# The experts' LayerNorm and routing moved into the attention's block, and dispatch's plan moved ahead of the places

## The reference

```python
x = x + _L0_attn_ref(_layernorm(x), Wq, bq, Wk, bk, Wv, bv, Wo, bo)
x = x + _L0_ffn_ref(_layernorm(x), gate_w, w_gate_proj, w_up_proj, w_down_proj)
x = x + _L1_attn_ref(_layernorm(x), w_in, w_param, w_out)
x = x + _L1_ffn_ref(_layernorm(x), lut, gate_idx, up_idx, down_idx)

# _L0_ffn_ref
router_logits = x @ gate_w.T
sel_w, sel_e = jax.lax.top_k(router_logits, 8)
masked = jnp.zeros((T, E)).at[rows, sel_e].set(softmax(sel_w))
h = silu(einsum('th,eih->tei', x, w_gate_proj)) * einsum('th,eih->tei', x, w_up_proj)
out = einsum('tei,ehi->th', h * masked[:, :, None], w_down_proj)
```

## Time and profile before

| | us |
|---|---|
| median of 3 runs (2475.92 to 2478.18) | 2477.4 |
| profiled execution, device time | 2489.67 |
| its span | 2488.2 |
| busy of the span: PE / DVE / ACT / POOL | 2283.7 / 1454.8 / 973.4 / 1083.1 |
| last addition of the projection ends | 606.5 |
| norm, first statistics to last low part | 622.1 to 650.9 |
| route, to the end of the mask | 651.7 to 671.9 |
| dispatch, to `token_of` | 672.2 to 708.6 |
| first transpose of the experts | 718.3 |

### The profile page before, as it was taken

The page is one execution under the profiler, slowest core; times in us unless marked ns, Lnnn a source line. Parts: engine busy times, 40 slices in busy tenths (PEclk is TensorE's granted clock), DMA queues, the critical chain, the costliest instruction groups (busy, mean ns, idle before and its releaser), DMA issues. The chain is left out here.

```text
span 2488.2 us, 45641 instructions
## 1 busy us (share of the span) xinstructions
PE 2283.7 (92%) x12486; PEld 1749.9 (70%) x12488; DVE 1454.8 (58%) x3393; ACT 973.4 (39%) x2177; POOL 1083.1 (44%) x976
## 2 busy tenths in 40 slices
PE   7989999967569999999999499999899998999998
PEld 5865555535359989988889278887766665788886
DVE  6446666634655555555555458998076665654554
ACT  3126666541444444444444332222365553312111
POOL 3128778877036666666667111111176662000000
PEclk9989999988679999999999699999999999999999
DMA  5469999987559999999998625456497841000001
GB/s 183 124 186 350 343 353 357 367 314 280 218 164 249 286 285 254 251 282 268 255 241 141 186 87 177 165 174 211 138 252 183 201 102 39 13 26 26 25 10 68
DMA packets 256541, 487.08 MB, mean 196 GB/s; under 512 B 32369, under 2 KB 149489, under 8 KB 246674
## 3 DMA queue, kind: packets, MB, share of 16 engines
q1 hardware_dynamic: 190418, 267.84, 35.2%
q0 software_dynamic: 62976, 212.42, 30.5%
q10 hardware_dynamic: 3024, 5.29, 0.6%
HBM read 588.77 MB, written 198.66 MB: 316 GB/s over the span
## 5 line engine op out<-in xcount | busy, mean ns | idle before, releaser
L1502 PE MATMUL m_ps_u<-m_ring,m_xT_hi 128*128 x1280 | 370.5, 350 | 0.7 <-issue 0.7
L1470 POOL DMA_INDIRECT expert_sum<-x_res,token_of x160 | 258.5, 1616 | 191.2 <-ACT x_res L1573 71.7
L1502 PEld LDWEIGHTS m_ps_u<-m_ring,m_xT_hi 128*128 128x128 f32 x1280 | 236.8, 190 | 1.8 <-issue 1.2
L845 ACT ACTIVATE probs<-ps_c 128x512 f32<-128x512 f32 (+3 forms) x384 | 176.7, 491 | 137.0 <-PE ps_c L771 94.3
L1502 PE MATMUL m_ps_u<-m_ring,m_xT_lo 128*128 x640 | 217.0, 339 | 0.0
L1463 POOL DMA_INDIRECT m_xg<-x_rows,token_of x160 | 171.4, 1072 | 85.1 <-issue 76.0
L1949 PE MATMUL s_ps<-s_x_hi,s_w_hi 128*128 128x512 f32 x512 | 200.4, 391 | 3.1 <-POOL s_w_lo L1919 3.0
L1949 PE MATMUL s_ps<-s_x_hi,s_w_lo 128*128 128x512 f32 x512 | 199.9, 391 | 0.0
L1949 PE MATMUL s_ps<-s_x_lo,s_w_hi 128*128 128x512 f32 x512 | 199.8, 390 | 0.0
L2718 DVE TENSOR_TENSOR x_res<-f_ps_o,x_res 128x512 f32<-128x512 f32 x176 | 109.3, 684 | 143.0 <-PE f_ps_o L2611 143.0
L1521 PE MATMUL m_ps_y<-m_ring,m_hT_hi 128*128 x480 | 176.6, 422 | 11.0 <-issue 11.0
(11 more groups left out here) (360 smaller groups left out, 5636.3 us busy)
## 6 DMA issues: line engine op xcount, KB each, us to landing
m_ring<-w_split SPq DMA_DIRECT2D x160, 1536.0 KB
m_ring<-w_split SPq DMA_DIRECT2D x160, 768.0 KB
w_split<-e_gu_parts POOLq DMA_DIRECT2D x32, 1536.0 KB, 7.5
proj<-s_out SPq DMA_DIRECT2D x32, 1024.0 KB, 3.9
e_raw_gu<-w_experts POOLq DMA_DIRECT2D x32, 768.0 KB
w_split<-e_dn_parts POOLq DMA_DIRECT2D x32, 768.0 KB, 7.1
e_raw_dn<-w_experts POOLq DMA_DIRECT2D x32, 512.0 KB
q_st<-q_parts SPq DMA_DIRECT2D x32, 256.0 KB, 6.3
```

The lines of the kernel that those rows point to most:

```text
L845: nc.scalar.activation(probs[a][j % RING][:, :width], ps_c[(j * BATCH + a) % BUFS][:, :width], ACT.Exp, scale=SCALE).then_inc(exp_done, 1)
L1470: pool.indirect_dma_start(acc[j % 2], rows_at(j), y[j % TURNS], None, bounds_check=PADDED - 1, oob_is_err=True, compute_op=ALU.add).then_i ...
L1502: last = nc.tensor.matmul(ps_u[b % 2][:, :W_UP], x[b % 2][:, k, :], ring[:, first + k * GU_ROW:][:, bass.ds(place, W_UP)], start=(n == 0), ...
```

## The change

The norm's own block goes. A new function, `project_and_normalize`, takes the place of `output_projection` in the attention's block: statistics of a group are taken between the steps of the next one, groups 0 and 1 are also normalized there, and the turning of all 16 tiles follows the last step, into three buffers that are the projection's own `ps_n`. The normalized rows lie in `m_xg`. `route` adds its code to the same block, with waits where a block's end stood, and the attention's semaphores are cleared behind it. In dispatch the plan is made before the places, the routing weights after the first marks, and their store is issued by ScalarE instead of SyncE.

```diff
@@ project_and_normalize, VectorE
+                if k == 0 and g >= 2:
+                    moments(g - 2)
+                if k == 1 and g > 0:
                     add(g - 1)
+                if k == 1 and g >= 2:
+                    scales(g - 2)
+                if k >= 2 and g > 0:
+                    for i in range(2):
+                        tile_stats((g - 1) * SUB + (k - 2) * 2 + i)
             low_part(len(STEPS) - 1)
-            add(GROUPS - 1)
+            moments(LAST - 1)
+            add(LAST)
+            scales(LAST - 1)
+            for i in range(TILES):
+                low_x(i)
+                if i < SUB:
+                    tile_stats(LAST * SUB + i)
...
@@ ScalarE
+                if at == 0 and group >= 2:
+                    deviations(group - 2)
+                if at >= 2 and group >= 2:
+                    for i in range(2):
+                        normalize((group - 2) * SUB + (at - 2) * 2 + i)
+            deviations(LAST - 1)
+            for i in range(TILES):
+                act.wait_ge(transposed, i + 1)
+                nc.scalar.copy(x_hi[:, :, toks(i)], ps_x[i % BUFS]).then_inc(x_hi_done, 1)
+                if i < SUB:
+                    normalize((LAST - 1) * SUB + i)
...
@@ TensorE
+            def turn(i):
+                pe.wait_ge(xn_ready, i + 1)
+                if i >= BUFS:
+                    pe.wait_ge(x_lo_done, i - BUFS + 1)
@@ route
         def _(pool):
+            pool.wait_ge(normalized.transposed, TILES)
+            pool.wait_ge(normalized.rows_stored, rows_stored_all)
             pool.memset(zeros[:, :], 0.0).then_inc(constants, 1)
...
+            pe.wait_ge(normalized.gw_lo_done, 1)
+            pe.wait_ge(normalized.x_lo_done, TILES)
...
+            dve.wait_ge(normalized.rows_stored, rows_stored_all)
             nc.vector.tensor_single_scalar(chosen[:, :, :], rest[:, :, :], TAKEN, ALU.is_equal)
@@ dispatch, ScalarE (and the same two lines gone from SyncE)
+                if i == 2:
+                    act.wait_ge(weighted, 4)
+                    act.dma_start(x_rows[:N_TOK, D:].rearrange("(n p) e -> p n e", p=P), routing[:, :, :]).then_inc(weights_stored, 16)
@@ mixture_of_experts
+            normalized = project_and_normalize(nc, block, sem, attended, x_res, ident, x_hi, x_lo, xn, gate_wT, gw_hi, gw_lo, x_rows[:, :D])
+            route(nc, block, sem, normalized, x_res, x_hi, x_lo, gw_hi, gw_lo, weight, chosen, ident, zeros, acc, x_rows, acc_ready, pads_ready)
+            attention_block.close()
```

More of the change, by code:

```diff
@@ L79, in load_tokens @@
     return x_loaded
[L82 to L223, removed]
-                    last.then_inc(transposed, 1)
@@ L227, in attention @@
-def attention(nc, x_in, x_res, x_loaded, ident, w, b_qk, b_v, wo, bo, w_raw, w_split):
+Attended = namedtuple("Attended", "yT all_sums wo_hi wo_lo wo_split in_chunk in_head of_head quarters y sums")
+def attention(nc, block, sem, x_in, x_res, x_loaded, ident, w, b_qk, b_v, wo, bo, w_raw, w_split):
     qk = {n: nc.dram_tensor(f"{n}_parts", (HEADS, 2, DH, 2 * BATCH + 1, GROUP), F32).ap()[:, :, :, :2 * BATCH, :].rearrange("h a d (s b) t -> h a d s b t", s=2) for n in "qk"}
@@ L256, in attention @@
                v_pair, probs, y_st, raw_wo, neg_max, both_max, max_cols, ident, ident_r, ident_bf, mask, mask_T, marks, warm)
-        output_projection(nc, block, sem, x_res, ident, yT, all_sums, wo_hi, wo_lo, wo_split, in_chunk, in_head, of_head, [q_0, q_1, k_0], probs)
+        quarters = [t[:, half, a, :] for t in (k_1, q_1, q_2) for half in range(2) for a in range(BATCH)]
+        y = [probs[0][0], probs[0][1], probs[0][2], probs[1][3]]
+        return Attended(yT, all_sums, wo_hi, wo_lo, wo_split, in_chunk, in_head, of_head, quarters, y, probs[1][2])
 Projected = namedtuple("Projected", "lo_done v_added hi_stored lo_stored stores k_sem k_count first_free all_done store_rest")
@@ L934, in _, with project_and_normalize @@
             evacuate(BODIES - 1, E - 1, 1)
-def output_projection(nc, block, sem, x_res, ident, yT, all_sums, wo_hi, wo_lo, wo_split, in_chunk, in_head, of_head, spare, spare_rows):
+Normalized = namedtuple("Normalized", "transposed x_lo_done gw_lo_done rows_stored")
+def project_and_normalize(nc, block, sem, attended, x_res, ident, x_hi, x_lo, xn, gate_wT, gw_hi, gw_lo, rows_out):
     SUB = GROUP // P
@@ L954, in output_projection @@
         ps_o = [ctx.enter_context(nc.psum_tensor(f"o_ps_o{b}", [P, D], F32)) for b in range(OUTS)]
+        ps_x = [t[:, :].rearrange("p (k t) -> p k t", k=KD) for t in ps_n]
         loaded = [sem(f"o_loaded{b}") for b in range(Y_BUFS)]
@@ L991, in project_tile @@
                     last.then_inc(step_done, 1)
+            def turn(i):
+                pe.wait_ge(xn_ready, i + 1)
+                if i >= BUFS:
+                    pe.wait_ge(x_lo_done, i - BUFS + 1)
+                for k in range(KD):
+                    last = nc.tensor.transpose(ps_x[i % BUFS][:, k, :], xn[:, i, k * P:(k + 1) * P], ident[:, :])
+                last.then_inc(transposed, 1)
             pe.wait_ge(rows_marked, 3)
@@ L1016, in _ @@
                 take_chunks(g)
-            for n, (group, _) in enumerate(STEPS):
+            for n, (group, at) in enumerate(STEPS):
                 act.wait_ge(y_ready, n + 1)
@@ L1044, in add, with tile_stats, moments, scales @@
                     nc.vector.tensor_tensor(x_res[:, i, :], ps_o[i % OUTS][:, :], x_res[:, i, :], ALU.add).then_inc(added, 1)
+            def tile_stats(i):
+                dve.wait_ge(added, i + 1)
+                nc.vector.bn_stats(stats[:, i, :], x_res[:, i, :]).then_inc(stats_done, 1)
+            def moments(g):
+                dve.wait_ge(stats_done, (g + 1) * SUB)
+                for i in range(g * SUB, (g + 1) * SUB):
+                    nc.vector.bn_aggr(mv[:, i, :], stats[:, i, :]).then_inc(aggregated, 1)
+                dve.wait_ge(aggregated, (g + 1) * SUB)
+                nc.vector.tensor_scalar_add(var_eps[:, of_group(g)], mv[:, of_group(g), 1], LN_EPS).then_inc(var_done, 1)
+            def scales(g):
+                dve.wait_ge(std_done, g + 1)
+                nc.vector.reciprocal(rstd[:, of_group(g)], std[:, of_group(g)]).then_inc(rstd_done, 1)
+                dve.wait_ge(rstd_done, g + 1)
+                nc.vector.scalar_tensor_tensor(shift[:, of_group(g)], mv[:, of_group(g), 0], -1.0, rstd[:, of_group(g)], ALU.mult, ALU.mult).then_inc(shift_ready, 1)
+            def low_x(i):
+                dve.wait_ge(x_hi_done, i + 1)
+                nc.vector.tensor_tensor(x_lo[:, :, toks(i)], ps_x[i % BUFS], x_hi[:, :, toks(i)].bitcast(F32), ALU.subtract).then_inc(x_lo_done, 1)
             rows = ident[:, :].rearrange("p (h a) -> p h a", a=CHUNKS)
@@ L1152, in mixture_of_experts, with route @@
     return acc, sums_ready
-def route(nc, x_res, x_hi, x_lo, gw_hi, gw_lo, weight, chosen, ident, zeros, acc, x_rows, acc_ready, pads_ready):
+def route(nc, block, sem, normalized, x_res, x_hi, x_lo, gw_hi, gw_lo, weight, chosen, ident, zeros, acc, x_rows, acc_ready, pads_ready):
     TAKEN = -3.0e38
```

118 lines of the change are left out of this document (76 added, 42 removed).

## The result

| | before | after |
|---|---|---|
| median of runs side by side | 2477.8 us (4) | 2450.7 us (4), 2448.4 to 2454.2 |
| ratio | | 0.9898, 95% 0.9878 to 0.9917 |
| profiled execution, its span | 2489.67, 2488.2 | 2451.83, 2450.3 |

By the medians it is 27.1 us faster, by the ratio 25.3 (forecast 2448.2, 29.2 won). The two profiled executions are 37.8 us apart. Of that, 7.5 is already there at the projection's last addition (606.48 before, 598.99 after); the last copy of attention, which no edit precedes, is 7.0 apart. From the addition to the start of dispatch 26.1 us are won, from there to the end of the experts nothing, and the last 4.3 lie behind the experts, where no edit is. Later times are therefore compared from that addition on.

What follows compares the result with a forecast made beforehand. The prediction took a serial chain ahead of the experts, not throughput, as the bound, including a wait for GpSimd. Its terms, 26.6 - 0.9 + 0 + 3.5 = 29.2 us, took 2477.4 to 2448.2 us, range 2441 to 2459.

Steps and rivals of the forecast that it cites:

- Norm and route: Between projection and dispatch: norm and routing inside attention's block start the route's TensorE code 26.6 us earlier, its length kept.
- rival 1: Norm's tail and logits: TensorE's clock stays high, tiles 1.0 and logit matmuls 2.0 us less, 2445 us; chance 0.17.
- Projection: Attention's output projection: norm work placed between its steps costs it 0 us.
- Rival 3: Projection: VectorE becomes its bound, 10.9 us of the gain gone, 2459 us; chance 0.05.
- Close: Between mask and dispatch: closing attention's long block takes 1.2 us instead of 0.30, 0.9 lost, bounds 0.5 and 3.4.
- Rival 2: Mask to first expert: the close costs its full 3.4 us and the gather's time is its own, 2454 us; chance 0.20.
- GpSimd off the path: Norm and route: the wait for GpSimd leaves the path; its splitting decides only when over 8 us late.
- rival 4: Norm to dispatch: splitting slips 15 us, zero fill and SyncE's stores end behind the mask, 2455 to 2465 us; chance 0.03.
- Plan and the experts' start: Dispatch and first expert block: the plan 6.2 us earlier lands the first gather sooner, 3.5 us won, bounds 0 and 4.3.
- The experts' clock: Experts' stage: stays 590 us at clock 1.00.
- rival 5: Experts' stage: less clock granted, gain gone at a mean of 0.95, 2492 us at 0.93; chance 0.05.

Runs made afterwards that it cites:

- e2: Kernel before with only dispatch changed (plan ahead of the places, weights' store on ScalarE's queue); ratio to before 0.9983.
- e1: Changed kernel with dispatch as before, so only norm and routing are changed; ratio to before 0.9893.
- e7: Changed kernel with GpSimd issuing 5 gathers ahead of the first scatter instead of 13; ratio to before 1.0908.
- e9: Changed kernel with 7 gathers, a wait for the first h, then two per scatter up to 13 ahead; ratio to before 0.9867, median 2451.1 us.
- e12: Changed kernel run once more, unedited; ratio to before 0.9896.
- e4: Changed kernel with GpSimd splitting only 8 columns of the experts' weights in its last turn; ratio to before 0.991.
- e6: Changed kernel with logits multiplied three matmuls at a time between the turnings of later tiles; ratio to before 0.9883, median 2448.5 us.
- e8: Changed kernel with both the early logits of e6 and the 5 gathers ahead of e7; ratio to before 1.0902.
- e5: Changed kernel with all norm work behind the last projection addition, still in attention's block; ratio to before 0.9925, median 2461.7 us.
- e10: e6 plus a GpSimd zero fill that waits for the first seven tiles' rows alone; ratio to before 0.984, median 2446.2 us.
- e11: e10 plus the gathers' train of e9 and GpSimd's long subtraction in three pieces; ratio to before 0.9868, median 2451.5 us.
- e3: Kernel before with GpSimd splitting only 8 columns of the experts' weights in its last turn; ratio to before 0.9953.

## Why the prediction was right, and where not

**Norm and route (26.6): right.** Last addition to mask takes 65.5 before and 38.1 after, 27.4 less; the mean over the traces with the same code there is 65.6 (before, e2) against 38.5 (after, e1, e7, e9, e12; 37.2 to 40.2), 27.1 less. Inside it two terms erred and cancelled in part. The last m_x_lo was put 18.5 us after the addition and came at 19.6, since the short shift operation took 1.62 instead of 0.16 and the normalizing behind it waited for it. The traces of the same code bear that out: with 0.17 in e4 the tail is 17.95, with 0.54 in e7 18.65, with 0.73 in e1 18.85, with 1.46 in e9 19.40, and with 2.35 and a second one of 1.14 in e12 21.77. The route, kept at 20.2 from the first logit matmul on, took 18.3: its logit matmuls start 0.23 apart at a granted clock of 1.00 instead of 0.43 at 0.50. In e1 the clock was 0.50 again from 619.5 to 622.9, among the logits, and last m_x_lo to mask took 20.1, so this part is not certain in every execution. So rival 1 came true in part: the clock stayed at 1.00 for the first tiles, was 0.50 from 603.2 to 616.8, where most tiles were turned as forecast, and 1.00 again under the logits.

**Projection (0): right.** TensorE is busy 17.90 of 17.90 us; VectorE's added work, 14.20 busy, fits, and the last two groups' additions start 11.46 us apart before and after. Rival 3 is out.

**Close (0.9 lost): 1.27 lost**, 1.57 or 1.58 for 0.30 in nine of the eleven traces that have it; in the other two (e6, e8) SyncE was still issuing. The term was put at 0.9 and is 0.4 larger. Rival 2's close of 3.7 is out; what the other 2.1 of its row were, the landing's report or something else, no run shows.

**GpSimd off the path: right** (last split store 606.54, zero fill at 617.29, e4). But rival 4's chain, zero fill to SyncE's stores, lay not far below: its last issue ended at 629.9, 7.1 us ahead of the mask's end, and early logits uncovered it.

**Plan and the experts' start (3.5): not confirmed.** Its first steps came as written: the metadata 6.7 us after dispatch begins, the ring's loads issued by 668.6, the first gather's rows 3.6 us after its issue instead of 7.8, first cast 4.3 sooner relative to dispatch. The step that failed is that a sooner first gather moves what follows. The 13 gathers start 1.32 us apart in a row, behind a token_of that did not come sooner (36.3 after dispatch began before, 36.6 after). ScalarE stood still until this train ended, and the eleventh block came 87.1 instead of 87.4 after dispatch began. Where ScalarE did not stand still the gain did reach the eleventh block: 80.6 in e5, with the early plan, against 85.8 in e1, with the late one, one trace each. What makes the standstill is open: it is missing with the shorter trains of e7 and e9, but also with the whole train of e5 and e6. And where it is missing, the end of the experts comes 691.2 to 699.1 after dispatch begins (without e7 and e8), where it is there 690.4 to 697.4: the stage's own waits vary by more (TensorE at the down products: 4.6 us in e1, 9.5 in after, 15.9 in e9). Whether any of the start's gain lasts is open; the whole change without this term would have been put at 25.7, and what was measured (20.6 to 30.2 by the ratio's interval) does not tell the two apart. The terms that did show add up to 26.1 in this trace, and 1.9 of that is the route's higher clock, which the forecast did not count on: so far the closeness of the total is luck.

**The experts' clock** is 1.00 as before; rival 5 is out.

## What to carry over

Work that waits only because a block must close gains that whole wait by moving into that block (e5: 17.1 us, block ends included); price the close (here 1.6 us) and look for the next queue that must drain before it. When a transfer is brought forward at the head of a long, DMA-bound loop, ask what paces the whole train and the loop, not when its first element lands: compare a mark ten iterations in, and the end, before believing the gain. Where executions differ by 10 us in parts that nothing touched, lengths between marks of one trace tell more than spans.

## What the runs showed of the hardware

- VectorE's shortest operations on SBUF took up to 20 times their length beside GpSimd's long ones. The shift (128x4, two inputs from SBUF) takes 0.16 or 0.17 with GpSimd idle (before, e4). It took 1.62 in after, from 599.10 to 600.72, beside GpSimd's subtraction from 597.24 to 600.70; 2.35 in e12 and 3.27 in e10, each ending 0.01 to 0.02 behind the subtraction; 0.92 in e11, with pieces of 1.3 us. GpSimd's cast held it too (0.73 in e1, 1.14 in e12). The reciprocal just before it (128x4, one input) took 0.17 inside the same subtraction, and four 128x512 additions with one input in PSUM took 2.48, as long as before. The Trainium skill (Advanced Engine Details and Errata, VectorE Performance Modes) says that VectorE's second port to SBUF is shared with GpSimd, and that GpSimd's instructions and those of VectorE that use both ports block each other. The traces agree that one waits for the other's end; which ports an operation used they do not show.
- ScalarE's standstill of 2.5 to 6.0 us ended with the train of gathers in before, after, e2, e3, e4, e10 and e12, 1.45 to 1.75 us behind the end of GpSimd's 13th gather instruction. It was absent with the shorter trains (e7, e8, e9, e11), but also in e5 and e6, whose gathers ran on while ScalarE worked; in e1 ScalarE came to that point only when the train was over. A fetch of instructions queued behind the gathers would be a guess, and the traced packets do not bear it out: in after no packet of the two instruction queues (63 of 16 KB and 60 of 8 KB in the whole run) moved from 687.9 to 695.3, and the next one, at 697.05, came behind the end of the standstill; nor did one move in that of e4, e10 or e12, while in before, e2 and e3 one began within it.
- Parts that no edit touched differed between executions: attention's last copy ended from 522.5 to 539.0 us, and the experts ended 690.4 to 699.1 us after dispatch began (without e7 and e8).
